# A decoder layer on one core: whole 128x128 products, TensorE's order without a loop, and two transposes by DMA

## What is computed

```python
x = x + attention(layernorm(x))              # 16 heads of 16, causal, W_qkv and W_out
x = x + cross(layernorm(x), ctx, mask)       # one head of 256: scores / 16, masked softmax, readout of ctx
x = x + ffn(layernorm(x))                    # two bit-linear layers, 256 -> 2 * 704 and 704 -> 256

def bit_linear(x, w, g):                     # rms norm, then 8-bit activations and ternary weights
    xn = rms_norm(x, g)
    xq = round(xn * 127 / max|xn|) scaled back
    wq = clip(round(w / mean|w|), -1, 1) scaled back
    return xq @ wq.T
h = gate * sigmoid(gate) * up                # between the two layers of ffn
```

## Time and profile before

| | us |
|---|---|
| time, median of 3 runs | 211.62 (211.55 to 212.03) |
| span of the profiled execution | 212.7 |
| TensorE products busy (PE) | 194.6, 91% of the span |
| TensorE weight loads busy (PEld) | 153.5, 72% |
| VectorE (DVE) | 165.7, 78% |
| ScalarE (ACT) | 150.6, 71% |
| GpSimd (POOL) | 137.1, 64% |
| granted TensorE clock, mean | 0.992 |
| moved by DMA | 12.8 MB |

### The profile page before, as it was taken

One profiled execution on the slowest core, in us unless ns is written; L12 is line 12 of the kernel. 1 busy time (PEld: TensorE's weight loads), 2 busy tenths in 40 slices (PEclk: granted clock), 3 DMA queues, 4 the chain that ended last, 5 costly groups with the idle time before them and its releaser, 6 DMA issues.

```text
span 212.7 us, 10882 instructions
## 1 busy us (share of the span) xinstructions
PE 194.6 (91%) x4104; PEld 153.5 (72%) x4107; DVE 165.7 (78%) x523; ACT 150.6 (71%) x422; POOL 137.1 (64%) x290
## 2 busy tenths in 40 slices
PE   4997999999999989999899989998999999889874
PEld 4785987978787868887787868787887866445532
DVE  1222587999988968798788888888879799999771
ACT  3468467767788886969587959887868866775821
POOL 4600341776758773948495857685755889999990
PEclk9998799999999999999999999999999999999999
DMA  5999000101010102020202011110101012000011
GB/s 172 379 330 348 25 3 6 52 3 51 6 49 30 53 6 74 0 76 2 76 0 74 2 28 48 32 44 25 51 25 51 24 52 77 0 5 26 2 43 59
DMA packets 11474, 12.79 MB, mean 60 GB/s; under 512 B 1009, under 2 KB 10801, under 8 KB 11442
## 3 DMA queue, kind: packets, MB, share of 16 engines
q1 hardware_dynamic: 11442, 12.41, 18.2%
HBM read 10.31 MB, written 2.10 MB: 58 GB/s over the span
## 4 chain that ended last, share of the span: by engine, by line
PE 72%; issue 10%; POOL 9%; DVE 4%; ACT 3%; DMA 1%; POOLq 0%; SPq 0%; DVEq 0%; ACTq 0%
PE ps L331 14%; PE ps L309 8%; PE ps L343 7%; PE ps L315 6%; PE ps L419 6%; PE ps L434 5%; PE ps L398 5%; PE ps L367 4%; PE ps L505 3%; PE ps L463 3%; POOL zh L1994 2%; PE ps L360 2%; PE ps L452 2%; PE ps L522 2%; PE ps L458 2%
## 5 line engine op out<-in xcount | busy, mean ns | idle before, releaser
L1994 POOL TENSOR_TENSOR zh<-hh,gd 128x352 f32<-128x352 f32 x32 | 31.2, 986 | 5.1 <-DVE hh L1331 4.7
L331 PE MATMUL ps<-yaT,wqk 128*128 128x128 f32 x256 | 32.9, 284 | 0.5 <-ACT yaT L681 0.5
L331 PEld LDWEIGHTS ps<-yaT,wqk 128*128 128x128 f32 x256 | 31.2, 199 | 1.2 <-ACT yaT L681 0.7
L1203 DVE TENSOR_REDUCE mx<-ps 128x16 f32<-128x1024 f32 x16 | 19.6, 1224 | 7.8 <-PE ps L367 7.6
L315 PE MATMUL ps<-wg,zT 128*128 128x352 bf16 x128 | 22.3, 312 | 0.5 <-ACT hT L681 0.4
L2016 POOL TENSOR_SCALAR hq<-zh,qh 128x704 f32<-128x704 f32 x16 | 13.6, 851 | 13.3 <-DVE qh L1360 13.0
L1910 POOL TENSOR_TENSOR rs<-ve,neghalf 128x1 f32<-128x1 f32 x32 | 20.2, 632 | 2.7
L681 ACT ACTIVATE hT<-ps 128x256 bf16<-128x256 bf16 (+1 forms) x32 | 15.5, 495 | 6.6 <-PE ps L309 6.5
L786 ACT ACTIVATE th_sb<-ps,th 128x352 f32<-128x352 f32 x32 | 17.4, 553 | 3.5 <-PE ps L315 1.8
L1318 DVE SCALAR_TENSOR_TENSOR th_sb<-th_sb,ps 128x352 f32<-128x352 f32 x32 | 16.4, 513 | 4.1 <-ACT th_sb L786 4.1
L738 ACT ACTIVATE pT<-ps 128x512 f32<-128x512 f32 x32 | 17.8, 609 | 1.3 <-PE ps L404 0.8
(11 more groups left out here) (120 smaller groups left out, 518.5 us busy)
## 6 DMA issues: line engine op xcount, KB each, us to landing
ct_in<-ctx_t SPq DMA_DIRECT2D x16, 128.0 KB, 2.1
cn_in<-ctx_n SPq DMA_DIRECT2D x16, 128.0 KB, 2.2
out<-o_out SPq DMA_DIRECT2D x16, 128.0 KB, 1.7
wg<-gate_t SPq DMA_DIRECT2D x1, 1408.0 KB, 7.7
x_in<-x SPq DMA_DIRECT2D x1, 1024.0 KB, 10.9
wd<-down_t SPq DMA_DIRECT2D x1, 640.0 KB, 8.7
wqk<-wqkv_t SPq DMA_DIRECT2D x1, 512.0 KB, 4.0
x_in<-x SPq DMA_DIRECT2D x1, 512.0 KB, 9.5
```

The costliest lines, as they stand in the source:

```text
L331: last = pe.matmul(qk_ps[:, e * P:(e + 1) * P], wqk[:, c, e * P:(e + 1) * P], yaT[:, t % 2, c, :], start=(c == 0), stop=(c == DC - 1))
L1203: V.tensor_reduce(out=mx[:, t % 2, :, 0, :], in_=scores, op=ALU.max, axis=AX).then_inc(ev["mx_d"], 1)
L1994: G.tensor_tensor(zh[:, t % 2, part], hh[:, t % 2, part], gd[:, part], ALU.mult).then_inc(ev[f"zh_d{j}"], 1)
```

## The change

1. `project_v` is two products of 128 x 256 per tile (four instructions) instead of eight. The output now has tokens on the partitions, so that `keep_v` copies v out with four instructions of 64x128 instead of two.
2. `cross_scores` computes all 128 x 128 scores of a tile, two products (four instructions), and adds the mask as a third product that also closes off the other sequence's keys. The masks of all tiles are made on GpSimd by two instructions at the start (`set_masks`) instead of one per tile. `cross_maxima` reads 128 columns instead of 64, the exponentials are one 128x128 instruction as before but without the doubled sum, and `keep_cross_weights` is one copy of 128x128 instead of two of 64x64.
3. TensorE's program has no loop: all steps are written out, in an order of their own, with constants in the waits. All tiles use the loop's form of `scores_q`, `scores_k` and `readout`. In `scores_q` the fixed products stand ahead of the wait for q and k, in `scores_k` part of them ahead of the wait for the transposed maxima, though most calls of `scores_k` still name `mT_d` among the waits at their start.
4. z and h are transposed by DMA from SyncE (`dma_start_transpose`), from SBUF to SBUF, 64 KB and 192 KB per tile. `transpose_z`, `transpose_h_0` and `transpose_h_1` leave TensorE, `keep_zT`, `keep_hT_0` and `keep_hT_1` leave ScalarE. SyncE's order is written anew with them in it; ctx of tiles 0 and 1 is loaded behind the weights and the last of x.
5. The orders on ScalarE, VectorE and GpSimd are rewritten around this; the operations in them are otherwise the same.

```diff
             def store(t):
                 sp.wait_ge(ev["out_d"], t + 1)
                 sp.dma_start(out[t, :, :], o_out[:, t % 2, :]).then_inc(stored[t % 2], 16)
...
+            def transpose_z(t):
+                sp.wait_ge(ev["zb_d"], t + 1)
+                after(sp, ev["gu_ps0"], t - 1)
+                after(sp, ev["gu_ps1"], t - 1)
+                sp.dma_start_transpose(zT[:, t % 2, :, :], zb[:, t % 2, :]).then_inc(zT_ld[t % 2], 16)
+
+            def transpose_h(t):
+                sp.wait_ge(ev["hb_d"], t + 1)
+                if t == 0:
+                    sp.wait_ge(pads_set, 3)
+                after(sp, ev["d_ps"], t - 1)
+                sp.dma_start_transpose(hT[:, t % 2, :, :], hb[:, t % 2, :]).then_inc(hT_ld[t % 2], 16)
...
+            transpose_h(4)
+            transpose_z(6)
             store(4)
             load_ctx(9)
+            transpose_h(5)
+            transpose_z(7)
             store(5)
...
+            transpose_z(15)
+            transpose_h(12)
+            transpose_h(13)
             store(12)
             store(13)
+            transpose_h(14)
+            transpose_h(15)
             store(14)
             store(15)
...
-                for b in range(2):
-                    for c in range(DC):
-                        for j in range(2):
-                            last = pe.matmul(v_ps[SEQ * j:SEQ * (j + 1), b * P:(b + 1) * P], yaT[:, t % 2, c, b * SEQ:(b + 1) * SEQ],
-                                             wv[:, c, j * P:(j + 1) * P], start=(c == 0), stop=(c == DC - 1))
+                for c in range(DC):
+                    last = pe.matmul(v_ps[:, :], yaT[:, t % 2, c, :], wv[:, c, :], start=(c == 0), stop=(c == DC - 1))
...
-                for rows in seqs:
-                    pe.matmul(sx_ps[rows, :], row_bf, mask_bf[:, t % 2, rows], start=True, stop=False)
                 for c in range(DC):
-                    for rows in seqs:
-                        last = pe.matmul(sx_ps[rows, :], yxT[:, t % 2, c, rows], ct_in[:, t % 2, c, rows], start=False, stop=(c == DC - 1))
-                last.then_inc(ev["sx_ps"], 1)
+                    pe.matmul(sx_ps, yxT[:, t % 2, c, :], ct_in[:, t % 2, c, :], start=(c == 0), stop=False)
+                pe.wait_ge(masks_0 if t < MASKS else masks_1, 1)
+                pe.matmul(sx_ps, row_bf, mask_bf[:, t, :], start=False, stop=True).then_inc(ev["sx_ps"], 1)
...
             def gate_up_0(t, *users):
-                pe.wait_ge(ev["zT_d"], at(t + 1))
+                pe.wait_ge(zT_ld[t % 2], 16 * (t // 2 + 1))
...
             def down(t, *users):
-                pe.wait_ge(ev["hT_d0"], at(t + 1))
-                pe.wait_ge(ev["hT_d1"], at(t + 1))
+                pe.wait_ge(hT_ld[t % 2], 16 * (t // 2 + 1))
...
-            with pe.Fori(0, TURNS) as turn:
-                for base in range(0, 9):
-                    at(Tile(base, turn))
-                for k in range(2):
-                    step(Tile(5 + k, turn))
-            kept.clear()
...
+            scores_q(10, ("exp_d0", 10))
+            transpose_cross_weights(7)
+            readout(9, ("out_d", 5))
+            cross_readout(7)
+            gate_up_0(6, ("mx_d", 11))
+            gate_up_1(6)
+            transpose_readout(9)
+            project_qk(11)
+            transpose_max(10, ("h1_d0", 7))
+            transpose_yx(8)
+            project_out(9)
+            cross_scores(8)
+            scores_k(10, ("hh_d1", 7), ("mT_d", 11))
+            project_v(11, ("expx_d", 9))
+            down(5, ("q_d", 12))
...
-                for j in range(2):
-                    rows = slice(SEQ * j, SEQ * (j + 1))
-                    last = copy(v2[rows, t % 2, :, :, j, 0:DK], v_ps[rows, :].rearrange("p (b i d) -> p b i d", b=2, i=PAIRS))
+                for b in range(2):
+                    for j in range(2):
+                        last = copy(v2[SEQ * j:SEQ * (j + 1), t % 2, b, :, j, 0:DK],
+                                    v_ps[SEQ * b:SEQ * (b + 1), j * P:(j + 1) * P].rearrange("p (i d) -> p i d", i=PAIRS))
...
-                for b in range(2):
-                    rows = slice(SEQ * b, SEQ * (b + 1))
-                    last = nc.scalar.activation(pxT[rows, t % 2, rows], pxT_ps[rows, rows], ACT.Copy, scale=2.0)
-                last.then_inc(ev["pxT_d"], 1)
+                copy(pxT[:, t % 2, :], pxT_ps).then_inc(ev["pxT_d"], 1)
...
```

More of the change, by code:

```diff
@@ L564, in _ @@
[L564 to L572 removed]
+            scores_k(1, ("mT_d", 2))
+            project_out(0)
+            scores_q(2, ("exp_d1", 2))
@@ new lines, in _ @@
+            transpose_yx(3)
+            project_out(4)
+            cross_scores(3)
+            scores_k(5, ("hh_d1", 2), ("mT_d", 6))
+            transpose_ya(7)
+            transpose_cross_weights(3, ("x1_d", 5))
+            down(0)
+            scores_q(6, ("exp_d0", 6))
+            readout(5, ("out_d", 1))
+            cross_readout(3)
+            project_v(6)
+            gate_up_0(2, ("mx_d", 7))
+            gate_up_1(2)
+            transpose_readout(5)
+            project_qk(7)
@@ new lines, in _ @@
+            transpose_yx(4)
+            project_out(5)
+            transpose_max(6, ("h1_d0", 3))
+            transpose_ya(8, ("yxT_d", 5))
+            cross_scores(4)
+            scores_k(6, ("hh_d0", 3), ("mT_d", 7))
+            project_v(7, ("expx_d", 5))
+            down(1)
+            transpose_cross_weights(4)
+            scores_q(7, ("exp_d1", 7))
+            readout(6, ("out_d", 2))
+            cross_readout(4)
+            transpose_yx(5)
+            gate_up_0(3, ("mx_d", 8))
@@ new lines, in _ @@
+            gate_up_1(3)
+            transpose_ya(9, ("yxT_d", 6))
+            cross_scores(5)
+            transpose_readout(6)
+            project_qk(8)
+            transpose_max(7)
+            project_out(6)
+            scores_k(7, ("hh_d0", 4), ("mT_d", 8))
+            transpose_cross_weights(5, ("x1_d", 7))
+            project_v(8)
+            down(2, ("k1_d", 9))
+            scores_q(8, ("exp_d0", 8))
+            readout(7, ("out_d", 3))
+            cross_readout(5)
+            transpose_yx(6)
@@ new lines, in _ @@
+            down(6, ("k1_d", 13))
+            transpose_cross_weights(9, ("x1_d", 11))
+            scores_q(12, ("exp_d0", 12))
+            readout(11, ("out_d", 7))
+            cross_readout(9)
+            transpose_ya(13)
+            gate_up_0(8, ("mx_d", 13))
+            gate_up_1(8)
+            transpose_readout(11)
+            project_qk(13)
+            transpose_max(12)
+            transpose_yx(10)
+            project_out(11)
+            cross_scores(10)
+            scores_k(12, ("hh_d1", 9), ("mT_d", 13))
@@ L2281 @@
     small[:, B_ID:B_ID + P] = np.eye(P)
-    small[0, B_ROW:B_ALL] = 1
+    for b in range(2):
+        small[b, B_ROW + SEQ * b:B_ROW + SEQ * (b + 1)] = 1
     for j in range(2):
@@ L2294 @@
     wv = wqkv[:, 2 * D:].reshape(D, PAIRS, 2, DK).transpose(0, 2, 1, 3).reshape(D, D)
+    mask = np.asarray(inputs["mask_BxS2_bk0"]).reshape(tiles, 2, SEQ)
+    own = np.zeros((2, tiles, P), mask.dtype)
+    for b in range(2):
+        own[b, :, SEQ * b:SEQ * (b + 1)] = mask[:, b]
     arrays = {
```

1562 lines of the change are left out of this document (759 added, 803 removed).

## The result

The changed kernel takes 218.70 us (median of 4 runs, 217.69 to 219.92) against 211.59: 1.0315 times the time before, 95% interval 1.0247 to 1.0382. It is **slower by 7.1 us**; 203 was forecast, with 0.16 for any slowdown.

What follows compares the result with a forecast made beforehand. TensorE was taken to bound the middle, chains through VectorE and GpSimd the end. Middle -7.6, before the loop -2.2 and end +1.3 sum to -8.5: span 212.7 gives 204.2, less 1.1 is 203.1, stated as 203; range 198 to 213.

Steps and rivals of the forecast that it cites:

- before the loop: Tiles 0 to 4: five shorter readouts (-1.85 us) and two z transposes off TensorE (-0.4), -2.2 us, range -0.5 to -3.5.
- the middle: Ten loop steps between the readouts of tiles 4 and 14: 10.45 us a step instead of 11.21, -7.6 us.
- the stall is no matter of the loop: Rival, chance 0.1: TensorE waits for instructions, not the jump, so written out the 3.8 us stay; 206 to 212 us.
- The loop, -0.38 a step: Ten loop steps: removing the back-jumps saves at most 0.38 us of TensorE idle time a step, 3.8 us over ten.
- Transposes off TensorE, -0.54 a step: Ten loop steps: z's transposes (0.20 us) and h's (0.12 and 0.22) leave TensorE, saving 0.54 us a step.
- half the gain: Rival, chance 0.15: transposes land in 2.8 to 3.6 us or VectorE's order leaves gaps; step about 10.85, total 208 us.
- v as whole products, nothing: v's products on TensorE: 1.09 us as sixteen instructions, 1.08 in the new form, so nothing won.
- Cross, +0.07 a step: Cross scores on TensorE: whole products take nearer 0.48 us instead of 0.41, 0.07 us more a step.
- L and the ring: Ten steps: z lands 2.3 us after its integers end; dependency cycle of 7.6 us plus that hides behind 10.4, costing nothing.
- slow-z rival: Rival, chance 0.15: z's DMA transposes late at `gate_up` every step; 214 us at 4.0 us landing, 224 at 4.6.
- The end, +1.3: From tile 15's readout on: DMA transposes uncovered, z net +0.4 us, h +0.9; +1.3 us, range 0 to +5.
- The base: Starting time for the total: the profiled span of 212.7 us, with the runs' median taken as 1.1 below it.

## Why the prediction was wrong, point by point

The sum was -8.5 and +7.1 came, 15.6 us apart. Two steps of the prediction made nearly all of it: "before the loop" was taken at -2.2 and came at +5.4, "the middle" at -7.6 and came at -0.6.

**"Before the loop, -2.2": failed, and with its sign.** It priced the first tiles by TensorE's own durations, 0.37 us for each readout, "where PE has hardly a gap". The readout in the small form is indeed shorter. But TensorE's waiting for its own instructions was put at nothing, and a form with more instructions stops more often. Up to the fourth tile the stretch came out +3.4, and its stalls add up to 3.40; the two forms exchanged give +9.6 in the one kernel and -3.1 in the other. That the stalls are waits for packets in the instruction queue is shown by their times (ends 1.20 to 1.55 us after a packet's); that more instructions bring more of them, by the two runs with the forms exchanged; that bulk loads can delay such a packet rests on one trace (5.22 us). How much of each stall is load and how much count was not taken apart.

**The rival "the stall is no matter of the loop"** had 0.1, and was right that TensorE waits for its instructions in written-out code: the earlier trace rows was the sign, a 1.41 us stall there. It was wrong for the loop's own stalls, which stand where no packet of instructions moves and go with the jump. I set it aside because 38 to 56 us showed none, and gave it 206 to 212, a loss of at most the 3.8 us that the loop's stalls cost. It had no term for more instructions making more stalls. In the execution of the earlier trace rows this had just cost 3 us: the `project_qk` behind it took 3.38 us, at half the clock.

**"The loop, -0.38 a step": failed.** Written out alone it gives 0.0. It took all of PE's 3.84 us of idle time for the jumps, of which only 2.6 are stalls without a releaser; in the changed kernel's ten steps 2.1 us of such stalls are back, four of them, each ending 1.1 to 1.6 us after a packet of instructions.

**"Transposes off TensorE, -0.54 a step": right on TensorE, wrong for the step.** PE's busy time came to 104.5 us in the ten steps; 103.6 were forecast. But ten steps took 112.1, 112.2, 111.4, 111.45 and 111.5 us in the kernel before, written out, with z, with h and as changed, with 104.5 to 110.0 us of PE busy. "The middle is bound by TensorE" with 3.4% idle was read as if all else would follow. What came up instead, by the changed kernel's waits on PE in the ten steps, columns: engine and line, what released it, total us, times, longest:

```profile
PE ps L413 <- DVE hh L1372: 2.3, 3, 0.9
PE ps L392 <- issue: 1.2, 2, 0.7
PE ps L472 <- DMA cn_in<-ctx_n: 0.6, 1, 0.6
PE ps L413 <- ACT kz L820: 0.5, 1, 0.5
PE ps L382 <- issue: 0.5, 1, 0.5
```

VectorE's `hh`, which frees the banks for `scores_k`, is the largest: the rival "half the gain" had such waits, at 0.15. I allowed 0.09 us a step for them. The step of the prediction that failed here is the sum for the middle, 10.36 a step and 10.45 with small waits: what TensorE no longer does came back as idle time (3.84 to 6.96 us), about a third of it stalls for instructions, most of the rest waits for VectorE, ScalarE and ctx. What holds the step near 11.15 us was not isolated and stays open.

**"v as whole products, nothing": right on PE** (0.97 against 1.02 us), while the kernel with that edit alone lost 5.2 us, 4.2 of them by the stall and the clock. Taking the edit back inside the changed kernel lost 11. So the form itself is not priced by either; where the stalls fall changes with any edit of TensorE's program.

**"Cross, +0.07 a step": right in the time.** Products of 0.50 us from start to start against 0.36, which is twice the term, but 0.05 to 0.09 us a tile in the time. The Trainium skill gives a speedup of up to 2 in "TensorEngine Tiling (Array Packing)", "Theoretical Speedup"; these rows show 1.4, so the rival by the full doubling (+0.41 a step) did not come.

**L and the ring, "nothing in the middle": right.** L is 2.4 us; 2.3 was taken. z is waited for at 49.38 (1.09 us), in none of the ten steps, and at the end for 0.16 and 0.89; h at the end for 0.19, 0.36 and 0.77. The slow-z rival's own step, a wait in every step, did not occur, though its range of 214 to 224 holds the time. The Trainium skill, "Advanced Engine Details and Errata", "X-Bar Transpose (TRN2)", has these DMAs as fast as regular ones. For landing the trace roughly agrees (64 KB in 2.4 us and 192 KB in 2.7, stores and loads of 128 KB in 1.9 to 3.1), but most issues of a transpose hold SyncE for 1.17 or 1.21 us, most plain ones for 0.33 to 0.58.

**"The end, +1.3": right** (+1.1). The credit for VectorE's new order was not isolated: z by DMA without that order costs 7.1 us there, but part of that is the clock.

**The base: misread, without harm.** "The runs' median is 1.1 below the span" compared executions of two kinds: time is span plus 1.9, and the median's span is 209.7. But to take 1.1 off is to start from the median, 211.6 - 8.5 = 203.1, which is the right base for a median. That it came out so is luck, since the 3 us lost in the profiled execution were not seen.

Not forecast at all: +2.0 between the fourth tile and tile 4's readout (z's 1.09, stalls 1.04) and +1.5 between the last two readouts, where ctx, loaded behind stores and transposes in SyncE's line, is waited for 1.07 us. With SyncE's order by readiness the ctx waits are gone; that kernel's median is 1.0 us lower, which the intervals do not resolve.

## What to carry to other kernels

Look at idle time that nothing releases, above all in the middle of a group, before pricing a form by its duration, and hold it against the packets of the instruction queue in the same trace: where they match, the number of instructions counts, and a form with fewer and longer ones can win although each readout costs more. An engine that is 97% busy is not thereby the only thing that sets a step; change one part alone, and see whether the step follows, before adding gains up. And before using one execution as the base, compare its span and clock with those of several.

## What the runs showed that I had not expected

- TensorE stalls of 1.1 to 5.2 us in the first 31 us stand in 14 of the 20 traces, and in 12 of them the clock goes to half behind them (not behind the 1.62 us in the changed kernel's profile): 16 products of `project_qk` in 3.2 to 3.5 us instead of 2.0. In the kernel before this comes and goes from execution to execution.
- These stalls end 1.20 to 1.55 us after a packet of 16 KB in the instruction queue has ended, and the earlier trace rows could have been read so before any experiment.
- Adding 88 instructions a tile to the first tiles costs 9.6 us, though each is shorter. The Trainium skill, "Runtime: NRT & Kernel Launch", "Instruction fetch mechanics", says that crossing from one 16 KB block of instructions to the next is mostly hidden and that kernels do well to unroll. The changed kernel's trace agrees with the first for most of its 33 packets, against ten stalls, but those cost 6.66 us; and unrolling the loop gave 0.9995.
- 32 spare DMA transposes, some 17,000 small packets, cost a kernel whose DMA engines are otherwise 12 or 13% busy in the ten steps 0.1 to 0.5%.
- Ten steps took 111.4 to 112.2 us in the kernel before, written out, with z, h or both by DMA, and as changed, whatever was taken off TensorE.
